# Turning du scaled by B instead of multiplying it by diagonals, in the last batch of a selective-scan kernel

## The reference, cut to what matters

```python
delta = softplus(dt_proj_w @ dt_lo + dt_proj_b)          # [batch, 1024 channels, 1024 positions]
def step(state, xs):                                       # over the positions
    d_t, B_t, C_t, u_t = xs
    dA = exp(d_t[..., None] * A)                           # 16 states a channel
    state = state * dA + (d_t * u_t)[..., None] * B_t[:, None, :]
    y_t = einsum('ben,bn->be', state, C_t)
y = (y + D * u) * silu(layernorm(x))
x = x + y;  x = x + ffn(layernorm(x))                      # base matmul + top-2 of 8 low-rank experts
```

## Time and profile before

| what | value |
|---|---|
| median of three runs | 2019.85 us (2019.84 to 2026.95) |
| the profiled execution, its own time | 2023.09 us |
| its span | 2021.3 us, 25834 instructions |
| PE busy | 1808.8 us (89%) |
| DVE busy | 1744.8 us (86%) |
| POOL busy | 1681.3 us (83%) |
| ACT busy | 1290.0 us (64%) |
| mean granted TensorE clock | 0.950 of 2.4 GHz |

### The profile page before, as it was taken

How to read it: one execution, slowest core, us unless ns; L and a number is a source line. 1 busy time by engine, 2 the same in 40 slices (tenths; PEclk the granted TensorE clock), 3 DMA queues, 4 the chain that set the end, 5 groups by cost and what they waited for, 6 DMA issues and landing times.

```text
span 2021.3 us, 25834 instructions
## 1 busy us (share of the span) xinstructions
PE 1808.8 (89%) x9000; PEld 1171.5 (58%) x9000; DVE 1744.8 (86%) x1397; ACT 1290.0 (64%) x1800; POOL 1681.3 (83%) x751
## 2 busy tenths in 40 slices
PE   8778888888788889899988899898999999989999
PEld 3346666666455555555555555565666666665554
DVE  3699999988999999999999999999999999995111
ACT  3485666666666676766676766666877777773332
POOL 0298999999998999999999999999999999997100
PEclk9889999998889999899999999999999999999999
DMA  4656666687786667697766676686676767666100
GB/s 160 213 199 211 218 209 205 211 298 268 240 283 215 217 201 223 219 311 256 250 221 218 205 230 212 213 299 224 233 226 225 227 227 224 226 228 246 57 31 32
DMA packets 158705, 435.01 MB, mean 215 GB/s; under 512 B 14608, under 2 KB 47632, under 8 KB 158576
## 3 DMA queue, kind: packets, MB, share of 16 engines
q1 hardware_dynamic: 155120, 420.79, 61.4%
q0 software_dynamic: 3456, 12.58, 3.2%
HBM read 382.46 MB, written 50.86 MB: 214 GB/s over the span
## 4 chain that ended last, share of the span: by engine, by line
DVE 38%; PE 31%; issue 15%; POOL 8%; ACT 6%; DMA 1%; DVEq 0%; POOLq 0%; SPq 0%; ACTq 0%
DVE state L1277 24%; DVE row L1259 9%; PE bank_a L642 6%; PE y_ps L586 6%; POOL prod L1419 5%; DVE conv L1251 3%; PE bank_b L642 3%; PE row L664 3%; POOL drive_rows L1412 2%; ACT decay L980 2%; PE row L580 2%; PE row L543 1%; PE bank_b L519 1%; PE bank_b L500 1%; ACT row L980 1%
## 5 line engine op out<-in xcount | busy, mean ns | idle before, releaser
L1419 POOL TENSOR_TENSOR prod<-state,c_rows 128x1024 f32<-128x1024 f32 x512 | 1209.5, 2393 | 101.1 <-PE y_ps L586 50.1
L1277 DVE TENSOR_TENSOR_SCAN state<-decay,row 128x1024 f32<-128x1024 f32 x355 | 808.8, 2283 | 21.0 <-PE row L580 13.5
L586 PEld LDWEIGHTS y_ps<-ident,prod 128*128 128x128 f32 x4096 | 488.0, 146 | 245.8 <-issue 158.7
L586 PE MATMUL y_ps<-ident,prod 128*128 128x128 f32 x4096 | 552.0, 282 | 46.2 <-POOL prod L1419 46.1
L642 PE MATMUL bank_a<-w_o,xnT 128*128 128x512 f32 x816 | 388.1, 606 | 12.3 <-DVE x L1324 12.3
L980 ACT ACTIVATE decay<-delta,a 128x1024 f32<-128x1024 f32 x355 | 397.3, 1137 | 1.5 <-DMA u_d<-decay 1.4
L1412 POOL TENSOR_TENSOR drive_rows<-du,b_rows 128x1024 f32<-128x1024 f32 x157 | 376.5, 2398 | 6.9 <-DMA b_rows<-bc_d 6.9
L1259 DVE TENSOR_TENSOR row<-du,row 128x1024 f32<-128x1024 f32 x296 | 358.1, 1210 | 25.1 <-PE row L543 24.8
L1277 DVE TENSOR_TENSOR_SCAN state<-row,drive_rows 128x1024 f32<-128x1024 f32 x157 | 357.3, 2276 | 19.3 <-POOL drive_rows L1412 15.5
L980 ACT ACTIVATE row<-delta,a 128x1024 f32<-128x1024 f32 x157 | 175.4, 1117 | 261.3 <-DVE state L1277 260.8
L543 PE MATMUL row<-parts,sel 96*128 96x512 bf16 x592 | 189.6, 403 | 80.7 <-DVE state L1277 74.3
(11 more groups left out here) (160 smaller groups left out, 1879.3 us busy)
## 6 DMA issues: line engine op xcount, KB each, us to landing
c_rows<-bc_d SPq DMA_DIRECT2D x512, 512.0 KB, 4.6
xrow<-in_x SPq DMA_DIRECT2D x32, 512.0 KB, 5.3
skip<-u_d SPq DMA_DIRECT2D x32, 512.0 KB, 8.8
yy_d<-yy SPq DMA_DIRECT2D x32, 512.0 KB, 6.5
u_d<-conv SPq DMA_DIRECT2D x24, 512.0 KB, 5.3
ctx<-u_d SPq DMA_DIRECT2D x48, 256.0 KB, 6.2
x<-in_x SPq DMA_DIRECT2D x24, 512.0 KB, 5.8
x<-yy_d POOLq DMA_DIRECT2D x24, 512.0 KB, 9.5
```

Of the source, the lines that this page charges most:

```text
L586: last = nc.tensor.matmul(y_ps[:, i * P:(i + 1) * P], source[:, i * P:(i + 1) * P], ident[:, :], start=(first and i % (H // P) == 0), stop ...
L1277: nc.vector.tensor_tensor_scan(state[:, q % STATES, :], factor, term, 0.0, ALU.mult, ALU.add).then_inc(scan_done, 1)
L1419: nc.gpsimd.tensor_tensor(prod[:, q % PRODS, :], state[:, q % STATES, :], c_rows[:, q % RING, :], ALU.mult).then_inc(prod_ready, 1)
```

## The change

In the last batch the matmuls with diagonals go. For a K step ScalarE now multiplies duT, group by group of 128 positions, by B's column (`scale_du`: eight activations of 128x128, with the scale taken from bT, four in each of two sections), into one of two buffers in w_in and w_x, which are free by then. TensorE turns the result back with eight transposes into the row (`times_b`). The K steps become 4, 8, 11 and 13, the P steps 1, 6 and 14; nine D steps stay. So step 11's drive leaves GpSimd, and its decay goes to the SBUF ring, made at section 9 in place of 10.

```diff
-DIAGONALS_AT = {(NBLK - NE - 1, 12): (B - 1, 4), (NBLK - NE, 2): (B - 1, 8), (NBLK - NE, 6): (B - 1, 13)}
...
-DIAGONALS = {0: (3, 5, 8, 10, 13), B - 1: (4, 8, 13)}
-ON_PE = [DIAGONALS.get(E // NE, ()) if E else () for E in range(NBLK)]
-POOL_ROWS = {0: (1, 6, 11, 14), B - 1: (1, 6, 11, 14)}
+DIAGONALS = {0: (3, 5, 8, 10, 13)}
+
+SCALED = {4: (1, 2), 8: (4, 5), 11: (6, 7), 13: (8, 9)}
+TURNED = dict(DIAGONALS)
+TURNED[B - 1] = tuple(SCALED)
+ON_PE = [TURNED.get(E // NE, ()) if E else () for E in range(NBLK)]
+POOL_ROWS = {0: (1, 6, 11, 14), B - 1: (1, 6, 14)}
...
+        def scaled(i):
+            return (w_in[:, :, :, :].rearrange("p i k c -> p (i k c)"), w_x[:, :, :].rearrange("p k c -> p (k c)"))[i % 2]
...
 def times_b(E, n):
-                pe.wait_ge(diagonal_ready, diagonals_before(b, n))
-                pe.wait_ge(duT_ready, 2 * T_BEFORE[E] + 2)
+                if b in DIAGONALS:
+                    pe.wait_ge(diagonal_ready, DIAGONALS[b].index(n) + 1)
+                    pe.wait_ge(duT_ready, 2 * T_BEFORE[E] + 2)
+                else:
+                    pe.wait_ge(scaled_ready, scaled_index(E, n) + 1)
                 pe.wait_ge(scan_done, q - 1)
                 for c in range(NE):
                     at = slice(c * P, (c + 1) * P)
-                    last = nc.tensor.matmul(row[n % 2][:, at], duT(E)[:, at], diagonal(b, n)[:, at], start=True, stop=True)
+                    if b in DIAGONALS:
+                        last = nc.tensor.matmul(row[n % 2][:, at], duT(E)[:, at], diagonal(b, n)[:, at], start=True, stop=True)
+                    else:
+                        last = nc.tensor.transpose(row[n % 2][:, at], scaled(scaled_index(E, n))[:, at], ident[:, :])
...
+            def scale_du(E, n, h):
+                i = scaled_index(E, n)
+                if h == 0:
+                    act.wait_ge(bT_ready, 2)
+                    act.wait_ge(duT_ready, 2 * T_BEFORE[E] + 2)
+                    if i >= 2:
+                        act.wait_ge(b_ready, R_INDEX[K_STEPS[K_INDEX[E, n] - 2]] + 1)
+                    else:
+                        act.wait_ge(x_ready, len(HALF_INDEX))
+                        act.wait_ge(us_used, (B - 1) * 2 * NE)
+                for c in range(h * NE // 2, (h + 1) * NE // 2):
+                    at = slice(c * P, (c + 1) * P)
+                    last = nc.scalar.activation(scaled(i)[:, at], duT(E)[:, at], ACT.Copy, scale=bT[:, c, n:n + 1])
+                if h:
+                    last.then_inc(scaled_ready, 1)
...
 # ScalarE's section(E, m), behind the decays, scale_skip and take_du, ahead of exp_gap, take_v, take_turned, take_gate
+                if b == B - 1:
+                    for n, at in SCALED.items():
+                        if m in at:
+                            scale_du(E, n, at.index(m))
...
-                if (E, m) in DIAGONALS_AT:
-                    make_diagonal(*DIAGONALS_AT[E, m], range(NE))
```

More of the change, by code:

```diff
@@ L69, in gate_at @@
     if E % NE == NE - 1 and E // NE + 1 < B:
-        return (5, 6) if E // NE + 1 in DIAGONALS else (4, 5)
+        return (5, 6) if E // NE + 1 in TURNED else (4, 5)
     return ((3, 4) if E < NE else (4, 5)) if ON_PE[E] else (2, 3)
@@ L75, in sizes_at @@
     if E % NE == NE - 1 and E // NE + 1 < B:
-        return (7, 8) if E // NE + 1 in DIAGONALS else (6, 7)
+        return (7, 8) if E // NE + 1 in TURNED else (6, 7)
     return ((1, 2) if E < NE else (2, 3)) if ON_PE[E] else (0, 1)
@@ L218, in program @@
         first_split = sem("first_split")
-        b_turned, bT_ready, diagonal_ready, du_turned, duT_ready = (sem(n) for n in (
-            "b_turned", "bT_ready", "diagonal_ready", "du_turned", "duT_ready"))
+        b_turned, bT_ready, diagonal_ready, du_turned, duT_ready, scaled_ready = (sem(n) for n in (
+            "b_turned", "bT_ready", "diagonal_ready", "du_turned", "duT_ready", "scaled_ready"))
         dt_ready, v_copied, delta_ready, du_ready = (sem(n) for n in ("dt_ready", "v_copied", "delta_ready", "du_ready"))
@@ L259, in diagonal @@
         def diagonal(b, n):
-            if b == 0:
-                return w_o[:, DIAGONALS[0].index(n), :]
-            return (b_rows[:, 1, :], b_rows[:, 3, :], conv[:, 0, :])[DIAGONALS[b].index(n)]
+            return w_o[:, DIAGONALS[b].index(n), :]
+        def scaled(i):
+            return (w_in[:, :, :, :].rearrange("p i k c -> p (i k c)"), w_x[:, :, :].rearrange("p k c -> p (k c)"))[i % 2]
         def duT(E):
@@ L268, in du_bank, with scaled_index @@
             return bank_a if E < NE and h == 1 else bank_b
-        def diagonals_before(b, n):
-            return (DIAGONALS[b].index(n) + 1 if n is not None else 0) + (len(DIAGONALS[0]) if b else 0)
+        def scaled_index(E, n):
+            return K_INDEX[E, n] - K_BEFORE[(B - 1) * NE]
         block = stack.enter_context(nc.Block())
@@ L730, in section @@
                     reduce_u(b + 1, 1, range(2 * m, 2 * m + 2))
-                if last and b + 1 in DIAGONALS and m == 4:
+                if last and b + 1 in TURNED and m == 4:
                     turn_b(b + 1, bank_b)
@@ L946, in make_diagonal @@
                 act.wait_ge(bT_ready, 1 if b == 0 else 2)
-                if b and 0 in cs:
-                    act.wait_ge(u_out[0], 16 * NBLK // 2)
-                    act.wait_ge(pool_drive, P_BEFORE[b * NE])
                 for c in cs:
@@ L1131, in section @@
                     split_first(b + 1)
-                if last and b + 1 in DIAGONALS and m == 5:
+                if last and b + 1 in TURNED and m == 5:
                     take_bT(b + 1, bank_b)
@@ L1439, in split_rest_of @@
                     pool.wait_ge(bc_out, 16 * (b + 1))
-                    if b in DIAGONALS:
+                    if b in TURNED:
                         pool.wait_ge(b_turned, 2)
```

## The result

The changed kernel takes 2043.05 us in the median of four runs (2041.89 to 2051.43), the kernel before 2022.44 (four runs, 2019.84 to 2026.95). The ratio is 1.0107, with a 95% interval of 1.0087 to 1.0127: slower by some 21 us. The forecast was 2023.7 with a range up to 2036. The profiled execution of the changed kernel was its slowest, 2051.43 us with a span of 2049.6, so its trace shows 28 us more than that of before. Of these only part lies in the last batch: from step 2 of block 24 to the gated sum of block 31 it took 426.0 us against 404.35 before. Another 6.7 us had already gathered by block 24, in code that is the same in both but for the diagonal in block 23, and the tails are within 0.1 us of each other.

What follows compares the result with a forecast made beforehand. VectorE was taken to set the pace, its work unchanged. Waits of +2.1 us and one TensorE clock fall of +1.7 made +3.8 us on 2019.85, so 2023.7 us, range 2014 to 2036.

Steps and rivals of the forecast that it cites:

- the last term of the sum: TensorE in the last batch: one clock fall in eight blocks, half rate on the chain to step 8, +1.7 us.
- the stretch ahead of the gate's second turn: TensorE waiting for the gate's copy: idle some 2.2 us instead of 0.47; whether the clock falls was left open.
- a second new stretch of about 1.9 us: TensorE idle before `experts`; in the clock rival up to 1.1 us more where it delays VectorE's add.
- that place: K steps other than 8, step 4 included: the shorter `times_b` lies off the path, no wait counted.
- the clock falls in most blocks: Rival: falls in six blocks of eight, 1.65 us each at step 8, +15 us, 2035 us; chance 0.22.
- The waits alone: All waits in the last batch without the clock: 8 x 0.3 + 7 x 0.05 - 0.6 = +2.1 us.
- the diagonal in block 23: Scan 14's wait of 1.25 us in block 23 goes, worth between 0 and 1.3; taken as -0.6 us.
- Prices: ScalarE and TensorE: half a scaled step 1.17 us, eight transposes end after 1.04 us.
- The routing copy: Step 6: copy moves to 1662.14, VectorE starts 0.66 us late; +0.31 us after the old wait's 0.35.
- The first add: VectorE waits 0.75 us for `experts`, nearly hidden by step 1's 0.70 us: +0.05 us a block.
- GpSimd's relief: Removing drive 11 ahead of product 10 wins nothing, since GpSimd then waits for scan 10; step 1's 0.7 us stays.
- Transposes and the clock: Transposes were expected to hold TensorE's clock; the rival that they don't: +24 us, 2044 us, chance 0.04.

Runs made afterwards that it cites:

- three scaled steps: Changed kernel with steps 4, 8 and 13 scaled, the last in sections 6 and 7, and step 11 back on GpSimd: 2029.28 us, ratio 1.0039.
- the filled version: Changed kernel plus sixteen zero-tile transposes ahead of `experts` and fourteen ahead of the gate's second turn: 2030.58 us, ratio 1.0048.
- The fourth diagonal: Kernel before the change, step 11 moved from GpSimd to TensorE by a diagonal made once, no scaling: 2025.6 us, ratio 1.0006.
- the last experiment: Kernel before the change plus twelve unread ScalarE activations in sections 8 and 9 of blocks 24 to 30, delaying gT: 2041.88 us, ratio 1.0095.
- three steps behind the gate's copies: Changed kernel with only steps 4, 8 and 13 scaled, behind gate and routing copies, step 11 on GpSimd: 2022.17 us, ratio 1.0002.
- the second mixed version: Changed kernel with steps 4, 9, 11 scaled behind the gate's copies, 13 by a diagonal, GpSimd's steps 1, 6, 8: 2027.49 us, ratio 1.0014.
- a third version: Changed kernel with only steps 4, 8 and 13 scaled, in sections 1, 2, 4 to 7, step 11 on GpSimd: 2029.28 us, ratio 1.0039.

## Why the prediction was wrong

**The step that failed** is the last term of the sum: "I count one fall in the eight blocks: +1.7 us". The clock went down eleven times in the profiled batch, and that cost some 18 us (the batch with both stretches filled is shorter by that; by the medians filling won back some 12). The count was the error, and with it the place. The prediction put the falls on the stretch ahead of the gate's second turn and called the one before `experts` "a second new stretch of about 1.9 us", worth "up to 1.1". In the changed kernel it was the reverse: the stretch ahead of `experts` was there (2.00 us in the undisturbed block, 1.83 to 3.38 in the others), and six of the eleven falls followed on it. The one at the gate was 1.70 us in that block, not 2.2, and only one fall followed on it, behind 2.39 us in block 31. In the version with step 13 by a diagonal it stood at 2.39 us in seven blocks without one fall; in the one with three scaled steps two of six such stretches had a fall behind them. Four more falls came around step 4, where TensorE waits 1.05 us for the first scaled buffer. The prediction put that place off the path and had no wait there.

It was the rival "the clock falls in most blocks" that happened, with a chance of 0.22 and a price of 15 us where the median shows 21. Its price per fall was not too low. Block 27, with one fall of 3.4 us, took 1.2 us more than the block without, and block 26, with one of 6.8 us, took 3.0 more; the price has 1.65. What it lacked is falls in every block but one, two of them in four blocks, and four that lasted twice as long. Behind the stretch ahead of `experts` TensorE works for 11 us without a pause until VectorE's second add (1814.35 to 1825.9 in block 30), with only 0.5 us to spare for what half rate loses.

**What held.**
- *The waits alone.* The prediction had blocks of 51.4 us with the clock up; the one block without a fall took 51.5, those of the filled version 51.3 to 51.6. The batch's waits, with one fall in block 24, cost 3.7 us. The sum said 2.1, of which -0.6 was for the diagonal in block 23: that came to nothing, since block 23 took 57.5 us in both kernels (VectorE's 1.25 us at scan 14 went, and its wait at drive 10 was 4.56 us instead of 3.50). Without it the term is 2.7, and 3.7 less the 1.0 us by which block 24 stands over the others comes to the same.
- *Prices.* Half a scaled step 1.17 us, eight transposes 1.04: as read from rows 4 and 5.
- *The routing copy.* 0.66 forecast (the prediction's own times, 1661.51 and 1662.14, give 0.63), 0.58 measured. *The first add.* 0.75 forecast, 0.94 measured, and step 1's wait took it up.
- *GpSimd's relief.* Costed at nothing. The fourth diagonal and the kernel without scaling show it; GpSimd waited 1.66 us ahead of product 10.
- *Transposes and the clock.* The Trainium skill, "TensorE: Matmul & The Clock Gate", Part 4, has it that transposes don't count as activity as matmuls do. No run here bears that out for these fp32 transposes: stretches filled with nothing but transposes held 1.00, and without scaling the batch ran at 1.00 on the same transposes.

**What stays open.** Which idle stretches bring the clock down. 2.39 us at the gate did not in seven blocks with step 13 by a diagonal, but did in two blocks with three scaled steps. Ahead of `experts` 2.00 us did not in block 30 of the changed kernel and 2.59 did not in block 24 of the last experiment, while 1.83 did in block 27 and 0.98 did twice with three steps behind the gate's copies. In the second mixed version it fell around waits of 1.29 us. So the length of one stretch doesn't decide it, and the number of falls in a run can't be forecast from it. The three runs beside the profiled one took 2041.9 to 2043.7 us; how their falls were spread isn't known.

## What to carry to other kernels

A wait that VectorE can hide may still cost by way of TensorE's clock: sum what becomes late for TensorE too, and price an idle stretch of about 2 us by what stands behind it at half rate until the next point where another engine waits, not by its own length. Before spending a spare engine's time, look at where in its queue the spare time lies; 13.9 us a block were free on ScalarE, but only a wait of 0.94 us of it lay between the row sum and gT. And a relief for an engine is worth nothing ahead of a place where it waits for another anyway; here only work taken from GpSimd behind scan 10 counted, in the second mixed version's blocks of 50.4 us.

## What the runs showed of the hardware

Putting 30 transposes that compute nothing into TensorE's queue (16 + 14 a block) made the changed kernel faster by 0.6%; in the trace the clock held at 1.00 from block 25 on. The same trick in the earlier batches raised the clock from 0.96 to 1.00 over 750 us and shortened that stretch by 6.3 us, which was lost again behind it, 4.6 us of it in the tail, with an idle stretch of 2.45 us and a clock fall that the tails of the 13 other traces don't have (save for falls in their last 2 us); the median didn't move. So what a clock is worth has to be read stretch by stretch, and a kernel with its clock held in one part can lose it in another. Under a fall the loss was 1.2 us for 3.4 us at half rate and 3.0 us for 6.8 (blocks 27 and 26 of the changed kernel). Blocks of 51.3 us with the same 2.39 us idle stretch in the same place kept the clock up every time, and blocks of 54.5 us with a stretch of 2.6 us or more lost it every time; in a third version the 2.39 us did both. The falls thus repeat from block to block where the blocks repeat, but no run here shows what decides them.
